# Key positions of even tiles, the order of the first loads, and unread TensorE products ahead of unit 0

## The reference, cut to what matters

```
x  = layernorm(hidden)                                  # 4 x 1024 x 512
q  = rope(rmsnorm(x @ Wq + bq)); lk = rope(rmsnorm(x @ Wlk + blk)); lv = x @ Wlv + blv
entries = softmax-weighted means of each 4 tokens       # 256 per sequence
ck = rope(rmsnorm(entries @ Wk + bk)); cv = entries @ Wv + bv
sparse: top 8 of q . ck (causal), softmax over them, times cv
local:  q . lk over the token's own block of 128 and the block before it, masked, softmax, times lv
out = hidden + ((sparse + local) * 0.5) @ Wo + bo + fp8(x) @ fp8(W2)
```

## Time and profile before

| what | value |
|---|---|
| median of 3 runs | 2570.6 us (2570.27 to 2572.04) |
| the profiled execution's own time | 2572.98 us |
| its span | 2571.2 us |
| TensorE busy | 2525.6 us, 98% |
| VectorE, ScalarE, GpSimd busy | 77%, 64%, 61% |

### The profile page before, as it was taken

The page is one execution under the profiler, slowest core; times in us unless marked ns, Lnnn a source line. Parts: engine busy times, 40 slices in busy tenths (PEclk is TensorE's granted clock), DMA queues, the critical chain, the costliest instruction groups (busy, mean ns, idle before and its releaser), DMA issues. The chain is left out here.

```text
span 2571.2 us, 54972 instructions
## 1 busy us (share of the span) xinstructions
PE 2525.6 (98%) x15288; PEld 2223.4 (86%) x15320; DVE 1985.2 (77%) x6309; ACT 1655.2 (64%) x4674; POOL 1569.2 (61%) x2768
## 2 busy tenths in 40 slices
PE   7999999999999999999999999999999999999998
PEld 5878888888888888888888888888888888888887
DVE  6888888888877778777877777877877776676775
ACT  4666666566666666666666666666666666666665
POOL 5777777776676555555556655555556655555554
PEclk9999999999999999999999999999999999999999
DMA  3531333223332212022243122121243221122101
GB/s 108 169 101 62 106 103 108 91 71 131 116 132 87 81 61 91 30 97 81 80 147 120 42 87 87 59 87 62 68 132 120 83 71 63 38 71 70 61 11 50
DMA packets 168291, 220.74 MB, mean 86 GB/s; under 512 B 17842, under 2 KB 89012, under 8 KB 167988
## 3 DMA queue, kind: packets, MB, share of 16 engines
q1 hardware_dynamic: 167268, 216.60, 25.7%
q10 hardware_dynamic: 720, 0.62, 0.1%
HBM read 156.35 MB, written 60.82 MB: 84 GB/s over the span
## 5 line engine op out<-in xcount | busy, mean ns | idle before, releaser
L1290 POOL TENSOR_TENSOR t<-raw,tB 128x128 f32<-128x128 f32 x512 | 227.9, 467 | 594.1 <-DVE raw L924 593.6
L1244 POOL TENSOR_TENSOR r<-ss,mh 128x4 f32<-128x4 f32 x256 | 286.8, 1120 | 261.2 <-DVE ss L941 261.2
L774 ACT ACTIVATE ch<-bVC,blT 128x128 fp32r<-128x128 f32 x512 | 160.3, 364 | 438.3 <-PE bVC L589 437.5
L514 PE MATMUL bQK<-wh,xh 128*128 128x512 f32 x1024 | 428.5, 418 | 0.8 <-DVE raw L924 0.8
L515 PE MATMUL bQK<-wl,xh 128*128 128x512 f32 x1024 | 405.4, 396 | 0.0
L516 PE MATMUL bQK<-wh,xl 128*128 128x512 f32 x1024 | 403.9, 394 | 0.0
L969 DVE CUSTOM_DVE_ANT_0 P<-bS,cst 128x256 f32<-128x256 f32 (+1 forms) x512 | 203.8, 398 | 159.4 <-PE bS L563 158.8
L530 PE MATMUL bVC<-wh,xh 128*128 128x256 f32 x1024 | 310.4, 303 | 4.9 <-DVE cl L1018 4.9
L741 ACT ACTIVATE P<-P,nm,r 128x256 f32<-128x256 f32 (+1 forms) x512 | 296.1, 586 | 0.0
L735 ACT ACTIVATE raw<-raw,r 128x128 f32<-128x128 f32 x512 | 178.4, 396 | 176.8 <-POOL r L1244 172.0
L532 PE MATMUL bVC<-wh,xl 128*128 128x256 f32 x1024 | 289.0, 282 | 0.0
(11 more groups left out here) (146 smaller groups left out, 6960.3 us busy)
## 6 DMA issues: line engine op xcount, KB each, us to landing
wh<-kept SPq DMA_DIRECT2D x144, 256.0 KB, 4.0
wl<-kept SPq DMA_DIRECT2D x144, 256.0 KB, 4.5
kept<-wh SPq DMA_DIRECT2D x48, 256.0 KB, 3.1
kept<-wl SPq DMA_DIRECT2D x48, 256.0 KB, 3.4
woh<-kepto SPq DMA_DIRECT2D x48, 256.0 KB, 3.4
wol<-kepto SPq DMA_DIRECT2D x48, 256.0 KB, 4.0
out<-acc SPq DMA_DIRECT2D x32, 256.0 KB, 3.1
ini<-in_hidden_states SPq DMA_DIRECT2D x24, 256.0 KB, 4.2
```

What stands on the lines that cost most here:

```text
L514: e.matmul(bQK[:, :], a, b, start=kt == 0, stop=False)
L1244: e.tensor_tensor(r4[:, u % 4], ss[:, u % 4], mh[:, 0:4], ALU.pow).then_inc(S["r4"], 1)
```

## The change

Even units' keys go to slot 2 and odd units' to slot 1. The order of blocks in units_of and the masks follow. For i = 0 the product begins at column 128 (first_key), so it multiplies slot 2 and the 32 compressed keys: 160 columns in place of 288. The clearing of slot 2 and its signal are gone. The constants are issued by SyncE behind the rows of tile 1, with the signal d_c for them alone; wcb and bcm have a new signal d_g, and wcb is issued before bcm. TensorE waits for d_c only; VectorE waits for d_g in step -8 and for d_c in step -7, and computes with the scale values in step -8 in place of -7. TensorE gets keep_busy: products of a tile of minus ones with itself, 128 x 128 in plain fp32, into bP[0], which nobody reads; 18 ahead of the first wait for the constants, and 2 after logits, 2 after entries and 5 where a step has a turn_x and no entries.

```diff
 def units_of(u):
-    return [u] if u % 8 == 0 else [u, u - 1] if u % 2 == 0 else [u - 1, u]
+    return [u] if u % 8 == 0 else [u - 1, u] if u % 2 == 0 else [u, u - 1]
...
+def first_key(u):
+
+    return 128 if u % 8 == 0 else 0
...
         def qk_of(w, u):
 
-            p = u % 2 + 1
+            p = 2 - u % 2
             return w[:, :, 0:p + 1:p, :]
...
         def mask_of(u):
-            a = C_MK + 128 * (u % 2)
+            a = C_MK + 128 * (u % 8 > 0 and u % 2 == 0)
             return cst[:, a:a + nloc(u)]
...
             load_acc(0)
             load_acc(1)
+            e.dma_start(cst[:, :], consts).then_inc(S["d_c"], 16)
             load_acc(2)
...
                     if u == 0:
-                        e.wait_ge(S["old"], 1)
                         e.wait_ge(S["eg"], FIRST_TILES)
...
-                n = 256 + C
+                a, b_ = first_key(u), 256 + C
                 q_, ql_ = qkh[:, h, 0, :], qkl[:, h, 0, :]
-                kh = qkh[:, h, 1:5, :].rearrange("p a c -> p (a c)")[:, 0:n]
-                kl = qkl[:, h, 1:5, :].rearrange("p a c -> p (a c)")[:, 0:n]
-                e.matmul(bS[h][:, 0:n], q_, kh, start=True, stop=False)
-                e.matmul(bS[h][:, 0:n], q_, kl, start=False, stop=False)
-                e.matmul(bS[h][:, 0:n], ql_, kh, start=False, stop=True).then_inc(S["s"], 1)
+                kh = qkh[:, h, 1:5, :].rearrange("p a c -> p (a c)")[:, a:b_]
+                kl = qkl[:, h, 1:5, :].rearrange("p a c -> p (a c)")[:, a:b_]
+                e.matmul(bS[h][:, a:b_], q_, kh, start=True, stop=False)
+                e.matmul(bS[h][:, a:b_], q_, kl, start=False, stop=False)
+                e.matmul(bS[h][:, a:b_], ql_, kh, start=False, stop=True).then_inc(S["s"], 1)
...
-            e.wait_ge(S["d_c"], 16 * 3)
+            def keep_busy(n):
+
+                for _ in range(n):
+                    e.matmul(bP[0][:, 0:128], minus1[:, :], minus1[:, :], start=True, stop=True)
+
+            e.wait_ge(S["ones"], 1)
+            keep_busy(18)
+            e.wait_ge(S["d_c"], 16)
             for s in range(FIRST, 0):
                 if tile_at(s, "turn") is not None:
                     turn_x(tile_at(s, "turn"))
                     logits(tile_at(s, "turn"))
+                    keep_busy(2)
                 if tile_at(s, "et") is not None:
                     entries(tile_at(s, "et"))
+                    keep_busy(2)
+                elif tile_at(s, "turn") is not None:
+                    keep_busy(5)
                 if block_at(s, "kv") is not None:
                     ckv(block_at(s, "kv"))
...
             def diagonal(t):
                 e.wait_ge(S["wl"], t + 1)
+                if t == 0:
+                    e.wait_ge(S["d_c"], 16)
...
-            e.dma_start(bcm[:, :], bc(bcmp, 1)).then_inc(S["d_c"], 16)
-            e.dma_start(wcb[:, :], Wcmp.rearrange("n a -> a n").broadcast_to([128, 512])).then_inc(S["d_c"], 16)
-            e.dma_start(cst[:, :], consts).then_inc(S["d_c"], 16)
+            e.dma_start(wcb[:, :], Wcmp.rearrange("n a -> a n").broadcast_to([128, 512])).then_inc(S["d_g"], 16)
+            e.dma_start(bcm[:, :], bc(bcmp, 1)).then_inc(S["d_g"], 16)
...
-                e.tensor_tensor_reduce(P[:, u % 2, h, 0:nloc(u)], bS[h][:, 0:nloc(u)], mask_of(u), 1.0, GONE,
+                e.tensor_tensor_reduce(P[:, u % 2, h, 0:nloc(u)], bS[h][:, first_key(u):256], mask_of(u), 1.0, GONE,
...
-                if s == FIRST + 2:
+                if s == FIRST + 1:
                     e.wait_ge(S["d_s"], 16 * 2)
...
                 if s == FIRST + 1:
-                    e.wait_ge(S["d_c"], 16 * 3)
+                    e.wait_ge(S["d_g"], 16 * 2)
+                if s == FIRST + 2:
+                    e.wait_ge(S["d_c"], 16)
...
-            e.memset(f32(qkh[:, :, 2, :]), 0.0)
-            e.memset(f32(qkl[:, :, 2, :]), 0.0).then_inc(S["old"], 1)
             e.memset(minus1[:, :], -1.0)
```

## The result

The changed kernel takes 2567.8 us (median of 22 executions, 2566.79 to 2570.52), the one before 2571.24 in the runs beside it (22, 2568.86 to 2574.95). The ratio is 0.9986, interval 0.998 to 0.9992: 3.4 us less, within the 0.2% that I called no change. The forecast was 2568.7, which is 1.9 us under the 2570.6 that it set out from. That the total is near says little by itself: it is a sum of terms of both signs, so each has to be looked up. A ratio is an estimate from all executions, and can differ by up to 0.0008 from the quotient of the two medians.

The account below looks back on a forecast made before the run. It took TensorE's in-order matmul queue to bound the steady part, with a start at the lower clock. Span 2571.2 - 6.1 + 4.0 + 0.2 = 2569.3, plus 1.8, less 2.4, gives 2568.7 us; range 2559 to 2577.

Parts of the forecast that it names:

- -6.1 for the products: Score products of i = 0: 192 products cut from 288 to 160 columns save 6.1 us.
- +4.0 for the unread ones: Start: unread products on TensorE at the lower clock delay the steps before unit 0, net loss 4.0 us.
- +0.2 for loads: Start: constants moved to SyncE's queue, later loads issued one issue later; loss between 0 and 0.45, taken as 0.2 us.
- the 0.100 us that I took: Price of one 160-column score product, a floor seemingly set by its 128-column weight load; before, 0.132 us.
- The other estimate, 10.2 us: Score products: saving if only the stream counts, 69 ns for 160 columns against 122 for 288.
- Rival (b): Score products: the stream alone prices the narrow product at 0.075 us, total 2563.9 us; chance 0.14.
- Rival (d): Score products: the narrow product leaves the fast rate, total 2576 us as one record, 2603 as two; chance 0.14.
- the lower clock at tile 1: Start: after the first 18 unread products a pause of 2 to 3.5 us leaves TensorE at the lower clock.
- the 4.96 us of every step -6 to -3: Start, tile 1 to tile 5: each step lengthened by four unread products at the lower clock, together +4.3 us.
- The lateness expected at unit 0: End of the start: unit 0's first product near 46 us in place of 40.34.
- Rival (a): Start: the clock rises early and holds, -4.5 us there, total 2560 us; chance 0.22.
- rival (c): Start: the filler never raises the clock, even with ckv; +8.3 us there, total 2573.0 us; chance 0.14.

Follow-up runs that it names:

- e5_224: Changed kernel without its unread products, i = 0 score products (from unit 8 on) widened from 160 to 224 columns; 2569.65 us, run once.
- e6b_half: Changed kernel without its unread products, i = 0 score products (from unit 8 on) with 64 of 128 query rows as weights; 2564.39 us, run once.
- e4_hold: Changed kernel plus 26 more unread products in the pauses of steps 0 and 1; 2567.27 us, ratio 0.9974 to the kernel before.
- e9_after_again: The changed kernel run again with no edit; 2569.07 us, ratio 0.9991 to the kernel before.
- e2_keys: Kernel before plus only the new key places and the narrow product, no unread products, old loads; 2568.01 us, ratio 0.9981.

## Why the prediction came out as it did

**The total was right with two terms off that in part cancel, and that is luck.** Forecast: -6.1 for the products, +4.0 for the unread ones, +0.2 for loads, together -1.9. Found: -4.1 by the steps (-3.4 by the rests), nothing that shows for the unread products inside the change (0.9986 with them, 0.9981 without, intervals that overlap), and 0 to +0.5 for the loads; measured together, -3.4.

**The narrow product.** The mechanism, a floor set by the weight load, was right, and e5_224 and e6b_half show it. Mis-sized is the price: the 0.100 us that I took was 0.112. The row was of 32-column records (0.097 us before rounding), and it was read as the price of a load alone. The other row, records of 128 streamed columns at 0.111, would have been the nearer one. Why a load beside only 32 streamed columns costs less, no run shows. The estimate from the Trainium skill's figure for the load ("TensorE: Matmul & The Clock Gate", "LDWEIGHTS (loading the stationary operand)"), 4.8 us saved, was nearer to the 4.1 found. The other estimate, 10.2 us by the formula of the Trainium skill, same page, "Back-to-back issue gap", took that formula further than the section does: it is given there for a single product by itself, and of a stream of loads and products the section says that both set the distance. The 0.112 us at 160 columns agrees with that. Rival (b), the stream alone, falls with the 0.074 that only appears at half the weights. Rival (d) falls with a single record at 0.112.

**The unread products.** The step that failed is "So whatever the first 18 give, I expect the lower clock at tile 1", and with it the 4.96 us of every step -6 to -3, which needs the lower clock until ckv. The clock was up at tile 1 (transposes in 0.63 us) and for about half of the time to 27.4, so tile 5 was late by 1.44 us and not 4.3. The price of a step at the lower clock was not far off: e4_hold, where the clock is down at tile 1, has steps of 4.7 us (16.32, 21.04, 25.73). But there too the filler brought the clock up long before ckv, at 27.9, and tile 5 was late by 1.8 us. In all five traces with early filler it was back at 22.8 to 28.7 us and stayed up to the end of unit 0's first half at least. Right was that ckv is delayed and runs at the full clock: it was 2.38 us late and made it good. The lateness expected at unit 0, near 46 us, was -0.35.

What I left out is the next step: with unit 0 faster, TensorE waits 2.40 us for ckr, which VectorE computes at its own pace, and the clock goes. Before, those products were slow and the wait was 0.9 us. The faster front became a longer pause, and the price of that pause is the rest of units 0 and 1 at half the clock. e4_hold, the changed kernel with the pauses filled, shows that it is the cause: unit 2 starts 4.5 us earlier. For how long the clock stays down is not fixed by the program: 17 us in this trace, 7 in e9_after_again. Rival (a) had the rise right and the holding wrong, rival (c) had neither.

**Loads, slots, clearing.** The loads were as reasoned: nothing to gain at the first weight chunk, a few tenths to lose. What the sum had no term for is the wait of 1.67 us for the scale values ahead of tile 0. Nothing in any run speaks for a price of the slots or the clearing: in e2_keys the median of each kind of step but that of an i = 0 is the kernel before's, within 0.003 us.

**The steady part.** That a shorter product comes out of the span one for one held: with TensorE busy all the time, eight units take 74.71 us in place of 74.84 (the sum of the eight median steps), where 74.6 and 74.8 were forecast.

## What to carry to other kernels

Price a narrowed product by the larger of its stream and its weight load: here 128 columns of weights cost 0.112 us, and nothing is gained by going from 224 columns to 160. Work put in to hold a clock belongs first in the pause just ahead of the work that is to profit, and a stage made faster lengthens the pause behind it: look there before adding up the gain. Where a start can come out in more than one way, one profile of each kernel decides nothing about 2 us; try each part alone, compare medians, and read a steady gain from the median of many like steps.

## What the runs showed of the hardware

- One program raised and lost the clock at different places of its start: the changed kernel's profile has it down from 44.4 to 61.5 us and unit 2 at 62.39, its repeat has it down from 45.8 to 52.6 and unit 2 at 59.75. In e2_keys it rose within ckv (2.56 us for eight records), in the kernel before, with the same work there, it did not (3.62).
- The granted clock in the profile is no witness until it first changes: in the kernel before it reads 1.00 from 0 to 31.4 us while the four transposes of a tile take 1.09 us, against 0.63 at the full clock. In the changed kernel it reads 1.00 up to 10.3 us, though the first 26 records stand 0.21 apart and the next nine 0.11.
- The same pause can keep or lose the clock: the 1.81 us of idle time in unit 9 (132 to 139 us) were followed by the lower clock in eight of fourteen traces.
- For fp32r the price of a product is flat from 160 to 224 columns at 0.112 us with 128 weight columns; with 64 weight columns and 160 streamed it is 0.074 us.
